# Storing the expert results expert by expert, and adding a whole quad in place: the tail of a language-model layer

## The reference, cut to what matters

```python
def _L0_ffn_ref(x, gate_w, gate_b, w1, w2):
    logits = jnp.einsum('bsd,ed->bse', x, gate_w) + gate_b
    probs = jax.nn.softmax(logits, axis=-2)
    vals, idx = top_k over the tokens, 8 for each of the 32 experts
    ...
    merged = jnp.einsum('bked,bke->bed', tok, vals)
    h = gelu(concat([merged, ones], -1) @ w1)      # per expert, 256+1 -> 1024
    o = concat([h, ones], -1) @ w2                 # per expert, 1024+1 -> 256
    out_tok = jnp.einsum('beo,bke->bkeo', o, vals)
    out = jnp.zeros_like(x).at[arange(b)[:, None], flat_idx].add(out_tok)
    return out
...
h = h + _L0_ffn_ref(_layernorm(h, axis=-1), ...)
```

## Time and profile before

| What | Value |
|---|---|
| Median of three runs | 889.64 us (888.16 to 892.07) |
| Span of the profiled execution, first to last instruction (the profile lists no other time for it) | 888.7 us |
| Median of the runs above that span | 0.94 us |
| Busy PE / DVE / ACT / POOL over the span | 80% / 69% / 40% / 51% |
| DMA rate over the span, and in the slices of the expert stage | 97 GB/s; 412 to 418 GB/s |
| Expert stage, first weight load of its own to last result copy | about 724.6 to 858.9 us |
| `combine`, chain of waits from its first semaphore to the end | 862.62 to 888.7 us |

### The profile page before, as it was taken

One profiled execution on the slowest core, in us unless ns is written; L12 is line 12 of the kernel. 1 busy time (PEld: TensorE's weight loads), 2 busy tenths in 40 slices (PEclk: granted clock), 3 DMA queues, 4 the chain that ended last, 5 costly groups with the idle time before them and its releaser, 6 DMA issues. The chain is left out here.

```text
span 888.7 us, 20544 instructions
## 1 busy us (share of the span) xinstructions
PE 710.7 (80%) x7708; PEld 478.2 (54%) x7708; DVE 617.1 (69%) x913; ACT 355.4 (40%) x561; POOL 452.7 (51%) x257
## 2 busy tenths in 40 slices
PE   3576759886999999999999999976899689875744
PEld 3354534444677777777777777755676323322221
DVE  3599947888999999999999999963676501100005
ACT  2366635353445545445455544433555211010100
POOL 1588700002999999999999999981111000000000
PEclk9799869998999999999999999987999879979765
DMA  5100000000001010000000000005800679999936
GB/s 109 48 1 0 0 1 0 0 0 14 8 14 38 13 35 12 11 7 12 12 12 12 12 12 8 12 14 198 313 25 1 233 271 412 417 416 416 418 135 213
DMA packets 48891, 86.34 MB, mean 97 GB/s; under 512 B 5232, under 2 KB 32432, under 8 KB 48848
## 3 DMA queue, kind: packets, MB, share of 16 engines
q1 hardware_dynamic: 43248, 81.23, 25.1%
q10 hardware_dynamic: 5600, 4.53, 1.6%
HBM read 76.31 MB, written 9.44 MB: 96 GB/s over the span
## 5 line engine op out<-in xcount | busy, mean ns | idle before, releaser
L898 POOL TENSOR_TENSOR read<-state,q_pos 128x1024 f32<-128x1024 f32 x128 | 300.2, 2365 | 28.5 <-DVE state L1007 22.4
L1007 DVE TENSOR_TENSOR_SCAN state<-fac,ps_up 128x1024 f32<-128x1024 f32 x128 | 290.1, 2278 | 8.6 <-ACT fac L942 8.2
L942 ACT ACTIVATE fac<-ps_xf 128x1016 f32<-128x1016 f32 x128 | 130.2, 1018 | 176.1 <-PE ps_xf L1041 160.2
L1041 PE MATMUL ps_xf<-hot,xtab 64*128 64x128 f32 x2048 | 148.4, 284 | 11.0 <-ACT fac L942 8.9
L1041 PEld LDWEIGHTS ps_xf<-hot,xtab 64*128 64x128 f32 x2048 | 125.4, 188 | 58.0 <-ACT fac L942 43.4
L1041 PE MATMUL ps_up<-hot,utab 64*128 64x128 f32 x2048 | 140.0, 276 | 19.3 <-DVE state L1007 19.3
L1041 PEld LDWEIGHTS ps_up<-hot,utab 64*128 64x128 f32 x2048 | 126.4, 189 | 24.9 <-issue 17.6
L907 POOL TENSOR_TENSOR utab<-tab 128x1024 f32 (+1 forms) x32 | 64.7, 2022 | 94.4 <-SPq L85 94.4
L1086 PE MATMUL ps_o<-read,sel 128*32 128x256 f32 x1024 | 82.4, 393 | 4.0 <-POOL read L898 4.0
L1627 DVE COPY h_t<-ps_ht 128x512 f32<-128x512 f32 x16 | 10.3, 686 | 75.7 <-PE ps_ht L1655 75.7
L997 DVE TENSOR_TENSOR xtab<-tab,ps_k 128x1024 f32<-128x1024 f32 x64 | 59.5, 930 | 1.5 <-PE ps_k L1033 1.5
(11 more groups left out here) (202 smaller groups left out, 995.0 us busy)
## 6 DMA issues: line engine op xcount, KB each, us to landing
w_sb<-in_L_ffn_w SPq DMA_DIRECT2D x32, 2048.0 KB, 19.4
rec_out<-osb SPq DMA_DIRECT2D x128, 32.0 KB, 1.5
ao<-rec_out SPq DMA_DIRECT2D x8, 512.0 KB, 4.4
out_dram<-res ACTq DMA_DIRECT2D x8, 512.0 KB, 2.8
tok<-in_x SPq DMA_DIRECT2D x2, 512.0 KB, 11.2
exp_out<-eo SPq DMA_DIRECT2D x8, 128.0 KB
oq<-exp_out SPq DMA_DIRECT2D x2, 512.0 KB, 3.9
w_nat<-in_L_tok_Wq SPq DMA_DIRECT2D x1, 256.0 KB, 3.1
```

What stands on the lines that cost most here:

```text
L898: nc.gpsimd.tensor_tensor(read[n % 2][:], state[n % 4][:].rearrange("p (b i t) -> p b i t", b=2, i=IB), q_pos[x.s][:, :, x.k].unsqueeze(2) ...
L942: nc.scalar.activation(fac[n % 2][:].rearrange("p (n t) -> p n t", t=T)[:, :, 1:], ps_x[:].rearrange("p (n t) -> p n t", t=T)[:, :, 1:], A ...
L1007: nc.vector.tensor_tensor_scan(state[n % 4][:], fac[n % 2][:], ps_u[n % 2][:], 0.0, ALU.mult, ALU.add)\
L1041: last = nc.tensor.matmul(dst[:, b * 512 + col * T:b * 512 + (col + 1) * T], stationary[rows], pos[rows], start=True, stop=True)
```

## The change

The diff, cut to its core. `exp_out` becomes [expert, sequence, feature], so that a group's store writes one contiguous block of 128 rows; `eo` shrinks from eight places to two, and VectorE waits for the store of group q - 2 before it writes place s again; the reload moves to the end of the expert block and becomes eight transfers, one for each half and each sequence-in-quad j, 32 partitions each. In `combine` one VectorE instruction adds all four results of a quad to `h2` in place; two stores of 256 KB send the quad out, one from SP and one from ScalarE's queue; `res` and the wait for its stores are gone, and the VectorE and ScalarE loops are written out.

```diff
-        m["exp_out"] = nc.dram_tensor("exp_out", [B, X, E], F32, kind="Internal").ap()
+        m["exp_out"] = nc.dram_tensor("exp_out", [X, B, E], F32, kind="Internal").ap()
...
+        m["oq"] = sb(life, "oq", [P, QUADS, E])
...
-    eo = sb("eo", [P, X // QB, E])
+    eo = sb("eo", [P, 2, E])
...
-            def store(q):
-
+            def store(i, s):
+
+                q = 2 * i + s
                 sp.wait_ge(eo_ok, START + q + 1)
-                sp.dma_start(exp_out[:, bass.ds(QB * q, QB)].rearrange("b x e -> x b e"),
-                             eo[:, bass.ds(q, 1)].rearrange("p i e -> p (i e)")).then_inc(eo_st, 16)
+                sp.dma_start(exp_out[bass.ds(QB * q, QB)].rearrange("x b e -> (x b) e"),
+                             eo[:, s]).then_inc(eo_st[s], 16)
+
+            def reload(h):
+
+                quads = slice(h * QUADS // 2, (h + 1) * QUADS // 2)
+                src = exp_out.rearrange("x (q j) e -> j x q e", j=QB)
+                for j in range(QB):
+                    sp.dma_start(oq[j * X:(j + 1) * X, quads], src[j][:, quads]).then_inc(f_ld[h], 16)
...
-            sp.wait_ge(eo_st, START + 16 * TURNS * 2)
+                store(TURNS - 1, s)
+            for s in range(2):
+                sp.wait_ge(eo_st[s], START + 16 * TURNS)
+            for h in range(2):
+                reload(h)
...
-                    nc.vector.tensor_copy(eo[:, bass.ds(2 * i + s, 1)], ps_2[s][:, 0:E].unsqueeze(1)).then_inc(eo_ok, 1)
+                    dve.wait_ge(eo_st[s], START + 16 * i)
+                    nc.vector.tensor_copy(eo[:, s], ps_2[s][:, 0:E]).then_inc(eo_ok, 1)
...
+        ps = [ctx.enter_context(nc.psum_tensor(f"ps_fo{s}", [P, QB, 512], F32)) for s in range(2)]
...
+        dst = out.rearrange("(q p s) t e -> q s t p e", s=2, p=2)
+
+        def stores(eng, s):
+            for q in range(QUADS):
+                eng.wait_ge(f_add, START + q + 1)
+                eng.dma_start(dst[q, s], h2[:, QB * q + 2 * s:QB * q + 2 * s + 2]).then_inc(f_out[s], 16)
+            eng.wait_ge(f_out[s], START + 16 * QUADS)
...
+            stores(sp, 0)
...
+            stores(act, 1)
...
                 if q % (QUADS // 2) == 0:
-                    pe.wait_ge(f_ld, START + (32 if q else 16))
-                pe.wait_ge(f_add[s], START + i)
+                    pe.wait_ge(f_ld[2 * q // QUADS], START + 16 * QB)
+                pe.wait_ge(f_add, START + q - 1)
...
-            with nc.vector.Fori(0, TURNS) as i:
-                for s in range(2):
-                    dve.wait_ge(f_mm[s], START + i + 1)
-                    dve.wait_ge(f_out[s], START + 16 * i)
-                    for j in range(QB):
-                        at = 2 * (j % 2) + j // 2
-                        last = nc.vector.tensor_tensor(res[s][:, at:at + 1], psx[s][j][:, 0:E].unsqueeze(1),
-                                                       h2[:, bass.ds(2 * QB * i + QB * s + j, 1)], ALU.add)
-                    last.then_inc(f_add[s], 1)
+            for q in range(QUADS):
+                dve.wait_ge(f_mm, START + q + 1)
+                rows = h2[:, QB * q:QB * (q + 1)]
+                nc.vector.tensor_tensor(rows, ps[q % 2][:, :, 0:E], rows, ALU.add).then_inc(f_add, 1)
```

More of the change, by code:

```diff
@@ L129, in tower @@
             recurrent_outputs(nc, a, m, sem, lambda n, s, d=F32: sb(mid, n, s, d), replace_tables)
+        m["oq"] = sb(life, "oq", [P, QUADS, E])
         with ExitStack() as last:
             experts(nc, a, m, sem, lambda n, s, d=F32: sb(last, n, s, d))
-        weights.close()
         combine(nc, m, sem, out)
@@ L1539, in experts @@
 def experts(nc, a, m, sem, sb):
-    ident, merged, exp_out = m["ident"], m["merged"], m["exp_out"]
+    ident, merged, exp_out, oq = m["ident"], m["merged"], m["exp_out"], m["oq"]
     w1, w2, b1, b2, w1_ld, w2_ld = m["w1_sb"], m["w2_sb"], m["b1_sb"], m["b2_sb"], m["w1_ld"], m["w2_ld"]
@@ L1553, in experts @@
         block = ctx.enter_context(nc.Block())
-        mq_ok, gl, ht, htok, eo_ok, eo_st = (
-            sem(n) for n in ("mq_ok", "gl", "ht", "htok", "eo_ok", "eo_st"))
-        l1, l2 = ([sem(f"{n}{s}") for s in range(2)] for n in ("l1_", "l2_"))
+        mq_ok, gl, ht, htok, eo_ok = (sem(n) for n in ("mq_ok", "gl", "ht", "htok", "eo_ok"))
+        l1, l2, eo_st, f_ld = ([sem(f"{n}{s}") for s in range(2)] for n in ("l1_", "l2_", "eo_st", "z_ld"))
+        m["f_ld"] = f_ld
         TURNS = X // QB // 2
@@ L1602, in second_weights @@
                     load_w2(sp, a, QB * (2 * i + s), h, w2[s], w2_ld[s])
-                store(2 * (i - 1) + s)
+                store(i - 1, s)
             first_weights(1, 0)
@@ L1615, in _ @@
             for s in range(2):
-                store(2 * (TURNS - 1) + s)
-            sp.wait_ge(eo_st, START + 16 * TURNS * 2)
+                store(TURNS - 1, s)
[3 more added lines that the diff above has]
+                reload(h)
         @block.vector
@@ L1689, in combine @@
 def combine(nc, m, sem, out):
-    h2, picked, exp_out = m["h2"], m["picked"], m["exp_out"]
+    h2, picked, oq, f_ld = m["h2"], m["picked"], m["oq"], m["f_ld"]
     with ExitStack() as ctx:
[L1693 to L1699, removed]
-        block = ctx.enter_context(nc.Block())
[L1702 to L1706, removed]
+        ps = [ctx.enter_context(nc.psum_tensor(f"ps_fo{s}", [P, QB, 512], F32)) for s in range(2)]
+        block = ctx.enter_context(nc.Block())
+        f_mm, f_add, f_out = sem("z_mm"), sem("z_add"), [sem(f"z_out{s}") for s in range(2)]
+        dst = out.rearrange("(q p s) t e -> q s t p e", s=2, p=2)
[4 more added lines that the diff above has]
+            eng.wait_ge(f_out[s], START + 16 * QUADS)
         @block.sync
@@ L1710, in _ @@
             m["start"](sp)
[L1711 to L1715, removed]
+            stores(sp, 0)
+        @block.scalar
+        def _(act):
+            stores(act, 1)
         @block.tensor
@@ L1720, in _ @@
             for q in range(QUADS):
-                i, s = divmod(q, 2)
                 if q % (QUADS // 2) == 0:
-                    pe.wait_ge(f_ld, START + (32 if q else 16))
-                pe.wait_ge(f_add[s], START + i)
+                    pe.wait_ge(f_ld[2 * q // QUADS], START + 16 * QB)
+                pe.wait_ge(f_add, START + q - 1)
                 for j in range(QB):
                     rows = slice(j * X, (j + 1) * X)
-                    last = nc.tensor.matmul(psx[s][j][:, 0:E], picked[rows, q], oq[rows, q], start=True, stop=True)
-                last.then_inc(f_mm[s], 1)
+                    last = nc.tensor.matmul(ps[q % 2][:, j, 0:E], picked[rows, q], oq[rows, q], start=True, stop=True)
+                last.then_inc(f_mm, 1)
         @block.vector
         def _(dve):
-            with nc.vector.Fori(0, TURNS) as i:
-                for s in range(2):
-                    dve.wait_ge(f_mm[s], START + i + 1)
-                    dve.wait_ge(f_out[s], START + 16 * i)
-                    for j in range(QB):
-                        at = 2 * (j % 2) + j // 2
-                        last = nc.vector.tensor_tensor(res[s][:, at:at + 1], psx[s][j][:, 0:E].unsqueeze(1),
-                                                       h2[:, bass.ds(2 * QB * i + QB * s + j, 1)], ALU.add)
-                    last.then_inc(f_add[s], 1)
[L1742 to L1751, removed]
+            for q in range(QUADS):
+                dve.wait_ge(f_mm, START + q + 1)
+                rows = h2[:, QB * q:QB * (q + 1)]
+                nc.vector.tensor_tensor(rows, ps[q % 2][:, :, 0:E], rows, ALU.add).then_inc(f_add, 1)
 _INS = ["x", "L0_tok_emb_W", "L0_tok_emb_b", "L0_tok_Wq", "L0_tok_bq", "L0_tok_Wk", "L0_tok_bk", "L0_tok_Wv",
```

## The result

The changed kernel takes 877.48 us in the median of four runs (874.81 to 877.77), against 889.5 us before. The ratio is 0.9857, with a 95% interval of 0.9836 to 0.9877: 12 us or 1.4% faster. The forecast was 878.9 us. The profiled execution is the fastest of the four, 874.81 us with a span of 873.1 us.

A forecast was written before the change was run, and what follows sets the result against it. It took late weights on four engines and final additions waiting for stores as bounds. Terms of -3.5, -1.2, -0.75, -5.5 and +0.2 sum to -10.75: span 888.7 to 877.95, plus 0.94 for the median, 878.9 us; range 875 to 883.8.

The forecast's parts named there:

- (a): Expert stage: result stores on sixteen engines instead of four no longer delay the last weights; -3.5 us, bounds 4.7 and 0.
- still narrow: Rival: the new result store also runs on few engines, so both store-shape gains are lost; 883.6 us, chance 0.11.
- (b): Last result store before the reload: its data take 0.4 us on sixteen engines instead of 1.6 on four; -1.2 us.
- The wait for a place: Expert stage: VectorE's copy of group q waits for the store of group q - 2; covered by over 3 us, no cost.
- (c): Reload as eight transfers issued right behind the last store's landing: TensorE starts earlier; -0.75 us, bounds 1.5 and -0.9.
- eight issues, then the meeting: Reload: SP's eight issues take 3.6 us, then engines meet in 0.34; TensorE starts 4.1 us after the last store lands.
- transfers one by one: Rival: the eight reload transfers run one after another, some 2 us each, losing reload and addition gains; 885.1 us, chance 0.07.
- (d): Final addition: transfers at 1.45 us a quad become the bound, 16.1 us from first matmul to end instead of 21.57; -5.5 us.
- slow halves: Rival: the two queues' 256 KB output stores take turns at half rate, 2.9 us a quad; 890.5 us, chance 0.04.
- (e): Head of the expert block: three more starting values, for which ScalarE waits; +0.2 us.

The follow-up runs named there:

- the eight wide kernels: The changed kernel and seven experiments, all traced with the 128x256 result store: mean 126.5 us from the first load to the last half of the second layer.
- one queue: Changed kernel with all sixteen 256 KB output stores issued from ScalarE's queue, none from SP: 877.98 us, ratio 0.9852 to the kernel before.
- the extra matmuls: Changed kernel with two unread 384-column matmuls added in TensorE's wait between the halves of the last group's second layer: 877.46 us.
- the half quads: Changed kernel with the final addition by 512-column half quads in four PSUM buffers, each with its own store, and the reload from two queues: 878.76 us.

## Why the prediction was right, step by step

- **Four engines late behind the weights (a)** was right in mechanism and size: -3.5 us forecast, -3.15 in the profiled pair, -3.55 against the mean of the eight wide kernels. The new shape does spread, as the forecast needed: the width was cut, undone and halved, and the tail went, came back, and came back in part (1.3 us of the 3.55). The rival "still narrow" is out.
- **The last store (b)** was mis-sized: -1.2 forecast, -1.65 measured. The term took only the data time out (1.6 to 0.4 us); the rest of the landing became shorter too (the issue alone from 0.56 to 0.33 us), and the store lands almost like one of 32 KB, near the far bound of -1.85 (1.5 us).
- **The wait for a place** costs nothing: every copy waited for matmuls alone. The cover was as forecast: landed by 756.5, wanted at 760.
- **The reload (c)**, forecast -0.75, gave -0.4. The forecast let two things end together, 4.1 us after the landing of the last store: the eight issues with the meeting of the engines behind them, and the landing of the first half. Both are there, and both take longer. In the changed kernel the transfers end last: the fourth lands 3.0 us after its issue, where 2.3 was taken, 4.41 us after the store. In four experiments with the same reload (the width undone, the addition undone, one queue, the extra matmuls) TensorE waited for SP's starting values behind the meeting, not for a transfer, and began 4.27 to 4.33 us after SP's first reload issue, against 4.38 in the changed kernel. So the step "eight issues, then the meeting" holds as one of two limits that are almost level, and halving the issues gained nothing because the other stayed. Why the reload moves at some 180 to 230 GB/s over its length in every form tried (206 and 222 inside the two halves of the kernel before) isn't shown. The rival of transfers one by one is out: eight of them land within 6.4 us of the last store.
- **The addition (d)** was mis-sized: -5.5 forecast, -6.25 measured, near the bound of 6.3. The term that was off is the pace of the output, taken as 1.45 us a quad from two lone stores; in an unbroken stream it is 0.524 MB / 381 GB/s = 1.38 us, and 8 x 0.07 = 0.56 us is most of the miss; the first store, 2.56 us after the first matmul instead of 2.7, is the next part. The rival "slow halves" (2.9 us a quad) is out with it. That transfers are the new bound agrees with the stream at a share of 1.08 and with the half quads, where a start 0.57 us earlier ended 0.57 us earlier and the stores took longer and longer to land. They are so by little: TensorE and VectorE alternate at 1.3 us a quad, as forecast.
- **The starting values (e)**, +0.2, can't be seen: from the first read of the recurrence to the first load of the expert block it takes 506.3 us, 506.6 before.

The misses of (b), (d) and (e), -1.4 together, are partly offset by those of (a) and (c), +0.7: that part of the agreement is luck. The steps sum to -11.45 where -10.75 was forecast, and the forecast of 878.9 lies 1.4 us above the median.

## What to carry to other kernels

When a queue carries bulk loads, look at the DMA share behind the last of them. Here a stretch at a quarter meant that small stores had run on a quarter of the engines, and that their time there, not their bytes, stood on the critical path. The cure was the shape of that transfer: with a first dimension of 32 or 128 instead of 4 the tail went, with 8 a third of its cost stayed. And a store that frees the buffer of the next result but one puts its whole latency into the loop, here 2.8 us for every two quads; adding in place, where the data allow it, turned the chain of latencies into a stream.

## What the runs showed of the hardware that was not expected

- Two issuing queues move the output no faster than one: 381 and 380 GB/s.
- The reload of 1 MB that was just written moves at some 180 to 230 GB/s over its length, while the output stores reach 381 and the weights 417 to 422. Longer rows and a faster issue brought TensorE's start no nearer, though the engines were up to 0.93 busy; the cause was not found.
- A lone store of 128 KB lands in 3.35 us as 4x32x256, in 2.6 as 8x16x256 and in 1.7 as 128x256.
- Half the matmuls bring no earlier start: VectorE's first addition begins 1.27 us after the first matmul with half quads (two matmuls) and 1.31 with whole ones (four).
